# Where a graph kernel builds its adjacency counts: 595 superslots dealt out differently over the slots of three layers

## What is computed

```python
x = x + L0(relu(layernorm(x)), edges, edge_attr_64)   # three transformer convolutions, log_softmax
x = x + L1(relu(layernorm(x)), edges)                 # ten steps of normed neighbour sums
x = x + L2(relu(layernorm(x)), edge_attr_32, edges)   # one normed sum with edge features
x = x + L3(relu(layernorm(x)), edges)                 # graph attention

# one convolution of L0, three times
kj    = k[src] + edge_attr @ We
alpha = sum(q[dst] * kj) / 8
w     = softmax of alpha over the edges of one dst
agg   = segment_sum((v[src] + edge_attr @ We) * w, dst)
x     = agg + x @ Ws + bs
```

## Time and profile before

| | |
|---|---|
| median of 3 runs | 4897.83 us (4896.31 to 4903.46) |
| the profiled execution | 4912.25 us, of which its span 4910.5 us |
| layers 0 and 1 | 97 to 1275 us and 1286 to 2466 us of the span |
| layer 2 | 2478 to 3637 us |
| L1 to L3 | the rest |
| PE, DVE, ACT, POOL busy | 72%, 66%, 49%, 51% |
| TensorE's granted clock | 0.794 of 2.4 GHz, mean |

### The profile page before, as it was taken

How to read it: one execution, slowest core, us unless ns; L and a number is a source line. 1 busy time by engine, 2 the same in 40 slices (tenths; PEclk the granted TensorE clock), 3 DMA queues, 4 the chain that set the end, 5 groups by cost and what they waited for, 6 DMA issues and landing times. The chain is left out here.

```text
span 4910.5 us, 91838 instructions
## 1 busy us (share of the span) xinstructions
PE 3513.1 (72%) x24220; PEld 3047.3 (62%) x24220; DVE 3256.5 (66%) x10240; ACT 2423.5 (49%) x8504; POOL 2498.9 (51%) x2591
## 2 busy tenths in 40 slices
PE   3677766666667666666657778777846999964887
PEld 2555555555555555555546667777746999962787
DVE  7677776777567776777737777777763333324996
ACT  0766666665376666666456666665421000000554
POOL 5777777674477777777267777777511000000000
PEclk9777888998578888988757888888757999975555
DMA  3444444442334444444144444444222000000001
GB/s 78 101 102 105 101 119 117 118 123 72 84 92 101 103 112 116 119 118 121 35 105 98 101 98 104 105 106 101 65 81 104 2 2 2 1 21 7 2 3 23
DMA packets 596225, 389.26 MB, mean 79 GB/s; under 512 B 441290, under 2 KB 518210, under 8 KB 595720
## 3 DMA queue, kind: packets, MB, share of 16 engines
q1 hardware_dynamic: 392839, 156.12, 12.5%
q0 software_dynamic: 81344, 84.68, 9.9%
q10 hardware_dynamic: 121536, 142.57, 9.8%
HBM read 315.36 MB, written 67.70 MB: 78 GB/s over the span
## 5 line engine op out<-in xcount | busy, mean ns | idle before, releaser
L615 POOL DMA_INDIRECT arena<-node_table,arena x1660 | 1603.2, 966 | 612.6 <-issue 467.8
L770 PE MATMUL ps<-arena 128*128 128x129 f32 x4980 | 948.3, 321 | 184.6 <-DVE arena L920 102.0
L679 ACT ACTIVATE arena<-arena 128x129 f32<-128x129 f32 x2490 | 742.8, 301 | 456.9 <-DVE arena L888 452.1
L770 PEld LDWEIGHTS ps<-arena 128*128 128x128 f32 x4980 | 791.0, 226 | 270.9 <-DVE arena L920 137.0
L917 DVE TENSOR_SCALAR arena<-arena 128x128 f32<-128x128 uint16 x2490 | 883.2, 360 | 94.7 <-PE ps L770 41.8
L615 POOL DMA_INDIRECT arena<-last_node_table,arena x830 | 794.1, 957 | 290.0 <-issue 233.5
L888 DVE TENSOR_TENSOR arena<-ps,arena 128x258 f32<-128x258 f32 x1245 | 524.3, 421 | 590.0 <-PE ps L759 247.9
L1165 PE MATMUL ps<-arena 128*128 128x192 bf16 x6875 | 589.6, 247 | 56.0 <-PEq L86 40.3
L1165 PEld LDWEIGHTS ps<-arena 128*128 128x128 bf16 x6875 | 587.4, 98 | 58.1 <-issue 52.3
L759 PE MATMUL ps<-arena,e 128*128 x2484 | 498.4, 332 | 113.4 <-DVE arena L888 56.5
L759 PE MATMUL ps<-arena 128*128 x2496 | 499.4, 333 | 103.6 <-ACT e L669 33.0
(11 more groups left out here) (324 smaller groups left out, 4705.8 us busy)
## 6 DMA issues: line engine op xcount, KB each, us to landing
arena<-in_attr SPq DMA_DIRECT2D x1245, 96.0 KB, 2.3
arena<-slot_rows ACTq DMA_DIRECT2D x249, 320.0 KB
edge_counts<-al ACTq DMA_DIRECT2D x397, 100.0 KB
arena<-node_table,arena POOLq DMA_INDIRECT x1660
edge_counts<-stage ACTq DMA_DIRECT2D x198, 100.0 KB
arena<-last_node_table,arena POOLq DMA_INDIRECT x830
arena<-edge_counts SPq DMA_DIRECT2D x24, 500.0 KB
stage<-edge_counts SPq DMA_DIRECT2D x16, 500.0 KB, 5.4
```

The costliest lines, as they stand in the source:

```text
L615: pool.indirect_dma_start(out=RING[:, t % R_SLOTS, XO:XO + XG], out_offset=None, in_=table[:, :], in_offset=bass.IndirectOffsetOnAxis(ap=I ...
L679: ins = act.activation(PR[j % 3][:, q], PR[j % 3][:, q], ACT.Copy, accum_out=AL[w % 2][:, c:c + 1])
L770: ins = pe.matmul(BPS[j % 2][:, 0:AB], WOH[j % 2][:, q], RING[:, r + q, D32:D32 + AB], start=q == 0, stop=q == BT - 1)
```

## The change

Two numbers of `adjacency_slots` and the two weights:

```diff
 def adjacency_slots(l, j):
 
-    light, last = 196, NBAT - 4
-    weigh = lambda k: 36 * min(k, light) + 100 * max(0, k - light) if l < 2 else k
+    light, last = 196, NBAT - 70
+    weigh = lambda k: min(k, light) + 2 * max(0, k - light) if l < 2 else k
     return share_weighed(ADJ_N[l], weigh(min(j, last)), weigh(min(j + 1, last)), weigh(last))
```

## The result

| | before | after |
|---|---|---|
| median | 4900.65 us (4896.31 to 4906.09, 4 runs) | 4867.97 us (4856.11 to 4872.11, 4 runs) |
| the profiled execution | 4912.25 us, span 4910.5 | 4856.11 us, span 4854.3 |

After is 0.9926 of before, with a 95% interval of 0.9907 to 0.9946: 36 us faster, 26 to 46 by the interval (the two medians lie 33 us apart). So some 23 us of what the two traces differ by is the choice of execution, and no stage can be held to a few microseconds by this pair alone.

The account below looks back on a forecast made before the run. No engine as a whole bound it: gathers paced light slots, the engines' own work paced slots from about 225. Layers 0 and 1 gain 50 - 22 = 28 us each, layer 2 gains 11: 67 us, 4831 us; range 4795 to 4880.

Parts of the forecast that it names:

- dear rival: Slots 196 to 344: serial stores and copies bind in every slot, 1.97 us a superslot, 20 us gained, 4878 us; chance 0.17.
- light slots paced by gathers: Layers up to about slot 196: POOL's gathers set about 2.5 us a slot, other engines have time to spare.
- Light, +37 at no cost: Slots 0 to 195, layers 0 and 1: 60 to 97 superslots, the added work lies under the gathers, costing nothing.
- Dense, +20 at 1.1 us: Slots 196 to 344, layers 0 and 1: 20 more superslots at 1.1 us each, 22 us later at slot 345.
- low bound: Dense slots: a superslot costs only its own 0.80 us on VectorE, 16 us a layer; not taken.
- Tail, -57, 50 us: Slots 345 to 414, layers 0 and 1: 57 superslots removed gain 50 us a layer, between 45 and 58.
- Layer 2, 11 us: Layer 2, windows 8 to 10: 14 superslots leave the path at 0.80 us each, 11 us; bounds 6 and 15.
- TensorE's clock falls in the tail: Tail: fewer matmuls drop the clock to 1.2 GHz, 30 us a layer lost, 4958 us; chance 0.06.
- Last product at most 25 us behind the last gather: Layers 0 and 1, sign of being right: last product at most 25 us behind the last gather, in place of 46.7.
- Tail at 155 to 166 us: Sign of being right: slots 345 to 414 take 155 to 166 us.
- Tail clock not below 0.7: Tail: a granted clock below 0.7 was named as a sign of being wrong.
- Windows 1 to 3 as long as before: Light windows 1 to 3, sign of being right: as long as now, the product still waiting for gathers.

Follow-up runs that it names:

- z2: Kernel before without feature loads once the ring is filled, superslots (light/dense/tail) 60/148/37 in layer 0, 117/128/0 in layer 1, 67/38/0 in layer 2: 4825.6 us, ratio 0.9861.
- z1: The changed kernel with its feature loads left out once the ring had been filled: 4811.6 us, ratio 0.9838 to the kernel before.
- z0: The kernel before with its feature loads left out once the ring had been filled: 4852.7 us, ratio 0.9928 to the kernel before.
- c1: The changed kernel with each count store to its own fixed place, not waiting for the one before, on a slow chip: 5916.3 us, ratio 0.9929 to the kernel before.
- 117/128/0: Light/dense/tail superslots in layers 0 and 1, layer 2 as in the changed kernel; against the kernel before on slow chips: 5964.5, 5965.3, 5965.1 us, ratios 1.0026, 1.0013, 1.0008.

## Why the forecast came true, and where it was off

The sign, the mechanism and the range held: 4868 us in 4795 to 4880. The size did not: 67 us were forecast, 36 came (26 to 46). 4868 also lies outside the band of 4812 to 4860 that had the chance of 0.58; the range holds it because it was drawn out to the dear rival's 4880, and by the time alone that rival is the nearest of all.

- **Premise: light slots paced by gathers.** Held on the chip of the result. VectorE's waits in windows 1 to 3 of layer 0 (213 to 561 us) answer to the earlier trace rows:

```profile
DVE arena L888 <- DMA arena<-node_table,arena: 46.6, 35, 3.1
...
DVE arena L888 <- PE ps L759: 10.4, 8, 3.7
```

  46.6 us of waiting for gathers where it was 61.4: the cover got thinner and did not go, and the three windows take 349.1 us where they took 350.9. On the slow kind of chip the premise is false; but what is lost there is above all the tail's return, 12 to 13 us in place of 50.
- **Light, +37 at no cost.** A little low. T225 is 4.2 and 6.3 us later, with 37 light superslots more ahead of it and three dense ones. z2's layer 1 prices 57 light ones alone at 8.3 us up to slot 345, 0.15 each, so 37 are about 5 (a single value, with a scatter of about 5 us).
- **Dense, +20 at 1.1 us.** This is the term that was mis-sized. Slots 225 to 344 grew by 26.3 and 29.1 us for 17 superslots, 1.5 and 1.7 each, and by 26.1 and 19.0 without loads, 1.5 and 1.1; the dense half alone cost 1.4 each. T345 came 30.5 and 35.4 us late where 22 were put, which lies inside the bounds of 16 to 39. The low bound was set aside because no slot would be left in which ScalarE catches up after a late landing, and then 1.1 was taken, close to it. The argument against the dear rival, that 103 of 120 slots already carried a store, speaks of a mean; the added ones cost more than that mean. That the 17 slots without one were where delays were made good is a reading that fits the first pair's waits (landings 9 us more, copies 15.5, expansion 17). It is not shown: z1's stretch grew by 26.1 us with no more waiting for landings than z0's (9.2 us against 10.2), c1 says nothing of single slots, and no run put single empty slots back.
- **Tail, -57, 50 us.** Right: 45.9 and 49.6 us (38.2 and 35.0 without the loads). The gathers take over as late next, as was worked out, but from a later start: the last gather moved back by 20 and 27 us with slot 345, which is how each microsecond of the dense stretch is passed on to the end.
- **Layer 2, 11 us.** Right in kind, and in size by z1 and z2, which gain 11.1 and 11.2. The 23.3 us between the first two traces go with a tail at 0.86 granted clock in place of 0.79:

```profile
3401.60:3593.00 191.40, 154.14 (x995) 142.10 (x994) 152.98 (x573) 86.45 (x336) 93.89 (x98) 0.79 0.29 64
```

```profile
3368.70:3536.20 167.50, 134.12 (x950) 126.15 (x948) 140.71 (x531) 79.77 (x322) 93.91 (x98) 0.86 0.29 65
```

  (Layer 2's tail, before and after: PE, PEld, VectorE, ScalarE, POOL busy with counts, clock.) z0, with the dealing of before, z1, with that of after, and z2 have it at 0.80, 0.80 and 0.81 in the same stretch, so the higher clock does not come with the dealing each time; it may be part of the 23 us named at the top.
- **Sum.** With the measured prices layers 0 and 1 give 57 x 0.84 - 20 x 1.5 - 37 x 0.15 = 12 us each, seen as 15.4 and 14.2 with loads and 10.7 and 15.6 without, and layer 2 gives 11. That is 36 to 41 us, in the measured 26 to 46.
- **The rivals.** "The dense stretch is dearer" was put at 1.97 us each, 20 us in all and 4878: its price is about as far above the measured 1.5 as the forecast's is below it, but its time is 10 us off where the forecast's 4831 is 37 off. Whether its mechanism, stores and copies that bind in every slot, is the right one stays open. "TensorE's clock falls in the tail" did not come about. Layer 0's tail, all engines as above, before and after:

```profile
1008.30:1219.50 211.20, 144.43 (x912) 116.51 (x912) 162.68 (x604) 129.75 (x480) 120.18 (x126) 0.88 0.39 97
```

```profile
1038.70:1203.90 165.20, 113.11 (x739) 98.35 (x739) 115.92 (x433) 102.73 (x422) 116.68 (x123) 0.87 0.38 88
```

  The granted clock is 0.87 with no superslot there, where it was 0.88. TensorE lost matmuls and the stretch got shorter with them, so that it is busy for 0.68 of the tail in both. The Trainium skill, "TensorE: Matmul & The Clock Gate", section "What's actually happening", says that activity releases the throttle; the rows agree as far as they go, since here neither the busy share nor the clock fell.
- **Signs named ahead.** Last product at most 25 us behind the last gather: 10.8 and 11.2. Tail at 155 to 166 us: 165 in both layers. Tail clock not below 0.7: 0.87. Windows 1 to 3 as long as before: 349.1 us against 350.9 (351.2 against 346.4 in layer 1). Slots 225 to 345 some 16 us longer: missed, 26 and 29. Dense slots over 2.75 us were the mark for "wrong": (347.1 - 18) / 120 = 2.74 in layer 0, just under it, and (348.2 - 18) / 120 = 2.752 in layer 1, just over.

What stays open: whether 117/128/0 beats the changed kernel where the kernel before takes 4900 us. Only one layer of z2 shows it, without the feature loads; three whole kernels of that dealing came to the slow kind of chip, where no dealing gains. Also open are what makes the added dense superslots dear, and what makes the slow chips slow.

## What to carry to other kernels

Price moved work by what the stage that receives it charges, and don't take that price from the mean pace of a stage that already carries the same work in most of its slots: the last slots filled can cost more than the mean. On the chip of the result and that of the z runs a superslot costs about 0.15 us under the gathers, 0.6 to 0.9 in the tail and 1.1 to 1.7 in the dense stretch, so one half of the change earned what the other half spent. And when two profiles differ by more than their medians, settle what a stage gained by a pair whose spans differ as their medians do.

## What the runs showed of the chip

- The same kernel took 4889 to 4901 us on the chip of the result and on that of the z runs, and 5951 to 5961 us on four. On those four the handoff ahead of one ScalarE copy took some 41 us against 4.74, light slots behind the first product 2.9 us against 2.4, dense ones 3.2 against 2.7. The nine profiled executions there had a mean granted clock of 0.728 to 0.745, against 0.792 to 0.809 in z0, z1 and z2. Emptying the tail gave 12 to 13 us a layer there against 34 to 50 on the other kind, and no dealing gained.
- The feature loads cost 37 us of 4890. In layer 0's dense stretch stores' landings were waited for 10.2 us without them and 24.1 with them.
- Without the wait of each count store for the one before (and with fixed addresses) the kernel took 38 us less than the kernel before, on a chip where that takes 5954 us.
- A count store of 100 KB held the next one back for 3.8 us (861.58 to 865.40) when a 320 KB row load was issued behind it on the same queue.
